# Routers of two sparse mixtures: gates on raw rows by tokens, mean and rstd applied to the logits, selection on logits, normalising on ScalarE

## The reference

```
# layer 1                                    # layer 3
logits = x @ gate_w + gate_b                 probs = softmax(x @ router_w.T)
vals, idx = top_k(logits, 2)                 gates, idx = top_k(probs, 2)
weights = softmax(vals)                      gates = gates / sum(gates)
h = relu(x @ w1[e] + b1[e])                  h = silu(x @ w1[e].T) * (x @ wgate[e].T)
out += weight * (h @ w2[e] + b2[e])          out += gate * (h @ w2[e].T)
```

## Time and profile before

| | us |
|---|---|
| median of three runs | 1674.88 |
| the profiled execution's own time | 1678.03 |
| span of its trace | 1676.3 |
| TensorE busy | 1599.8 (95%) |
| VectorE busy | 1241.1 (74%) |
| ScalarE busy | 932.0 (56%) |
| GpSimd busy | 290.5 (17%) |
| mean granted clock of TensorE | 0.984 |

### The profile page before, as it was taken

The page is one execution under the profiler, slowest core; times in us unless marked ns, Lnnn a source line. Parts: engine busy times, 40 slices in busy tenths (PEclk is TensorE's granted clock), DMA queues, the critical chain, the costliest instruction groups (busy, mean ns, idle before and its releaser), DMA issues.

```text
span 1676.3 us, 26239 instructions
## 1 busy us (share of the span) xinstructions
PE 1599.8 (95%) x8693; PEld 1247.8 (74%) x8693; DVE 1241.1 (74%) x2118; ACT 932.0 (56%) x1568; POOL 290.5 (17%) x270
## 2 busy tenths in 40 slices
PE   9998998999999998989999999999899999999998
PEld 8886766868866886468778765775588888888886
DVE  8827662464755474779999868552699999999997
ACT  1424473443624362139999744421387887887884
POOL 0014630010210021159100301000380000000003
PEclk9998997999999999989999999999999999999999
DMA  8010000022000002143853340005153528935003
GB/s 333 20 50 2 1 2 13 1 114 76 2 26 13 1 2 80 47 144 138 308 206 136 87 164 1 1 1 225 41 189 141 206 93 370 380 143 234 25 19 99
DMA packets 42240, 173.15 MB, mean 103 GB/s; under 512 B 10219, under 2 KB 10472, under 8 KB 26681
## 3 DMA queue, kind: packets, MB, share of 16 engines
q1 hardware_dynamic: 28742, 153.75, 23.9%
q0 software_dynamic: 8960, 10.29, 2.3%
q10 hardware_dynamic: 4464, 8.13, 1.3%
HBM read 275.54 MB, written 19.25 MB: 176 GB/s over the span
## 4 chain that ended last, share of the span: by engine, by line
PE 77%; DVE 13%; issue 3%; DMA 2%; ACT 2%; POOL 1%; SPq 0%; DVEq 0%; ACTq 0%; POOLq 0%
PE bank L1065 10%; PE bank L1069 10%; PE bank L1066 10%; PE bank L829 5%; PE bank L917 4%; PE bank L889 4%; PE bank L964 3%; PE bank L877 3%; PE bank L1013 3%; PE bank L1189 3%; PE bank L1297 3%; PE bank L848 2%; PE bank L1091 2%; PE bank L1271 2%; PE bank L840 2%
## 5 line engine op out<-in xcount | busy, mean ns | idle before, releaser
L710 POOL DMA_INDIRECT sb_W<-slots_out,sb_slus x20 | 29.9, 1494 | 541.7 <-DMA slots_out<-sb_rC 536.2
L785 PE MATMUL bank<-sb_ones 128*128 128x512 f32 x220 | 106.4, 634 | 8.8 <-DVE sb_rC L2584 6.3
L1505 ACT ACTIVATE sb_rF<-sb_rF,sb_nmx 125x625 f32<-125x625 f32 (+4 forms) x120 | 89.5, 746 | 45.1 <-DVE sb_nmx L2031 45.0
L652 POOL TENSOR_TENSOR sb_rstd<-sb_ve,sb_half 125x3 f32<-125x3 f32 (+3 forms) x23 | 22.9, 998 | 458.3 <-DVE sb_ve L1951 239.9
L384 DVE TENSOR_TENSOR sb_rA_r<-sb_W,sb_rA_r 128x1024 fp32r<-128x1024 f32 x68 | 83.5, 1227 | 12.2 <-ACT sb_rA_r L1602 12.0
L2031 DVE CUSTOM_DVE_ANT_0 sb_rF<-bank,sb_rG 125x625 f32<-125x625 f32 x80 | 61.5, 807 | 36.1 <-PE bank L877 35.2
L785 PEld LDWEIGHTS bank<-sb_ones 128*128 128x128 f32 x220 | 43.3, 203 | 59.9 <-issue 50.7
L384 DVE TENSOR_TENSOR sb_XT_r<-sb_W,sb_XT_r 128x1024 fp32r<-128x1024 f32 x68 | 83.4, 1226 | 0.0
L384 DVE TENSOR_TENSOR sb_rB_r<-sb_W,sb_rB_r 128x1024 fp32r<-128x1024 f32 x68 | 83.3, 1225 | 0.0
L1602 ACT ACTIVATE sb_rA_r<-sb_W 128x1024 fp32r<-128x1024 f32 x68 | 71.6, 1053 | 20.2 <-DMA sb_W<-in_w_m 17.5
L1637 ACT ACTIVATE sb_rG_r<-bank 128x512 fp32r<-128x512 f32 x51 | 30.6, 599 | 82.4 <-PE bank L1091 82.4
(11 more groups left out here) (534 smaller groups left out, 4780.1 us busy)
## 6 DMA issues: line engine op xcount, KB each, us to landing
sb_W<-in_w_m SPq DMA_DIRECT2D x204, 1024.0 KB
sb_rDE<-in_w_m SPq DMA_DIRECT2D x17, 1024.0 KB
sb_rC<-slots_in SPq DMA_DIRECT2D x33, 256.0 KB, 2.7
sb_W<-in_w_g SPq DMA_DIRECT2D x8, 1024.0 KB, 5.0
slots_out<-sb_rC ACTq DMA_DIRECT2D x31, 256.0 KB, 2.1
slots_in<-sb_rC SPq DMA_DIRECT2D x1, 4608.0 KB, 24.8
sb_W<-in_w_a SPq DMA_DIRECT2D x4, 1024.0 KB, 18.2
sb_W<-in_w_m SPq DMA_DIRECT2D x2, 2048.0 KB, 16.7
```

The costliest lines, as they stand in the source:

```text
L785: pe.matmul(bank[:, b, :], ones[:], ones[:, 0:1].broadcast_to([P, D]), start=True, stop=True)
L1505: act.activation(SM[:, s % 4, 0:kn], SM[:, s % 4, 0:kn], ACT.Exp, scale=-1.0, bias=nmx[:, s:s + 1], accum_out=dens[:, s:s + 1]).then_inc(S ...
```

## The change

For layers 1 and 3 alone:

- TensorE turns the raw rows `X` (`raw_gates`). Tile u's gates follow as soon as tile u is in `XT`, with tile u's 125 columns of `XT` standing still and the 8 columns of `gw` moving, so logits come out as rows. ScalarE copies all five tiles (`raw_tiles`).
- At router 0 TensorE multiplies ones by `gw` for the column sums, and VectorE keeps them in `gsum`.
- VectorE's `picks` takes out mean times `gsum`, multiplies by rstd, adds the bias (layer 1), and looks for the two best on the logits. The sums of `MK` wait for `MK` and no longer for `COMB`; exp takes LG minus the maximum, and `COMB` is made of exp and `MK`.
- ScalarE writes `XN` behind exp (`normal_rows`), and GpSimd's scatter waits for it.
- `chosen_nodes` goes tile by tile, each waiting for its tile of `SEL0`.
- VectorE's first low halves move behind `slots`; in stage 1 ScalarE's second high halves move ahead of `combT`.

```diff
+        gsum = sb("gsum", [R, 32])
...
-                pool.wait_ge(S("ln_vec"), LN[4 if r == 1 else 8] + STATS + T)
+                pool.wait_ge(S("x0"), ROWS_XN[r] + T)
...
+            def raw_gates(r, ready, base):
+
+                for t in range(T + 1):
+                    if t < T:
+                        pe.wait_ge(ready, base + t + 1)
+                        for c in range(C):
+                            mm = pe.transpose(bank[:, t, c * R:(c + 1) * R], X[:, t, c * P:(c + 1) * P], ident[0:R, 0:R])
+                        mm.then_inc(S("tr_full"), 1)
+                    if t >= 1:
+                        u = t - 1
+                        pe.wait_ge(S("x0"), ROWS_XT[r] + u + 1)
+                        for c in range(C):
+                            mm = pe.matmul(bank[0:R, 7, u * E:(u + 1) * E], XT[:, c, u * R:(u + 1) * R], gw[:, c, GW[r]:GW[r] + E],
+                                           start=(c == 0), stop=(c == C - 1))
+                mm.then_inc(S("rt_pe"), 1)
...
-                pe.wait_ge(S("rt_vec"), ROUTED[r] + ROUTER_OPS[r])
+                pe.wait_ge(S("rt_vec"), ROUTED[r] + PICKED[r])
...
-                def chosen_nodes(chosen):
-
-                    for k in range(C):
-                        for t in range(T):
+                def chosen_nodes(chosen, one_by_one=False):
+
+                    for t in range(T):
+                        if one_by_one:
+                            pe.wait_ge(S("sl_vec"), SLOT_OPS * (r // 2) + SELECTED - T + t + 1)
+                        for k in range(C):
                             mm = pe.matmul(bank[:, 6, k * P:(k + 1) * P], XN[:, t, k * P:(k + 1) * P], chosen(t),
-                                           start=(t == 0), stop=(t == T - 1))
+                                           start=(t == 0 and k == 0), stop=(t == T - 1), skip_group_check=True)
                     mm.then_inc(S("b_xt"), 1)
...
+                if c == 3:
+                    for k in range(C):
+                        pe.matmul(bank[0:R, 2, 0:32], ones[:, 0:R], gw[:, k, 0:32], start=(k == 0), stop=(k == C - 1))
...
-            routed_feats(4, 5, 1)
-            feats_ready(5)
+            raw_gates(1, S("lf_vec"), LF_OPS)
+            keep(5, 4)
...
+            def raw_tiles(r):
+
+                for t in range(T):
+                    act.wait_ge(S("tr_full"), T * (5 if r == 1 else 9) + t + 1)
+                    act.activation(XT[:, :, t * R:(t + 1) * R], bank[:, t, 0:C * R].rearrange("p (c n) -> p c n", c=C),
+                                   ACT.Copy).then_inc(S("x0"), 1)
+
+            def normal_rows(r):
+
+                act.wait_ge(S("ln_vec"), LN[4 if r == 1 else 8] + STATS + 1)
+                for t in range(T):
+                    act.activation(XN[:, t], X[:, t], ACT.Identity, scale=rstd[0:R, t:t + 1], bias=shift0[:, t:t + 1]).then_inc(S("x0"), 1)
...
-                act.wait_ge(S("rt_vec"), ROUTED[r] + (4 if r in (0, 2) else 3))
+                act.wait_ge(S("rt_vec"), ROUTED[r] + (5, PICKED[1] + 1, 4, PICKED[3] + 1)[r])
...
+                    normal_rows(3)
                     return
                 if r == 1:
-                    act.wait_ge(S("rt_pe"), 4 * r + 4)
+                    normal_rows(1)
+                    high_halves(1, ("a", 1), 0)
+                    act.wait_ge(S("rt_pe"), RT_PE[r] + 2)
...
-            feats(5, XT)
+            raw_tiles(1)
             high_halves(1, ("a", 0), 0)
-            logits(1)
             router(1)
-            high_halves(1, ("a", 1), 0)
...
+                if r == 0:
+                    c(dve.tensor_copy(gsum[:], bank[0:R, 2, 0:32]))
...
+            def picks(r):
+
+                k = 4 if r == 1 else 8
+                c = Chain(dve, S("rt_vec"), ROUTED[r])
+                means = bcast(mv[0:R, :, 0], E)
+                c(dve.tensor_tensor(EX[:], means, gsum[:, GW[r]:GW[r] + E].unsqueeze(1).broadcast_to([R, T, E]), ALU.mult))
+                c.sync()
+                dve.wait_ge(S("rt_pe"), RT_PE[r] + 1)
+                c(dve.tensor_tensor(LG[:], bank[0:R, 7, 0:T * E].rearrange("p (t e) -> p t e", t=T), EX[:], ALU.subtract))
+                c.sync()
+                dve.wait_ge(S("pow"), POW[f"ln{k}"])
+                c(dve.tensor_tensor(LG[:], LG[:], bcast(rstd[0:R, :], E), ALU.mult))
+                dve.scalar_tensor_tensor(out=shift0[:], in0=mv[0:R, :, 0], scalar=-1.0, in1=rstd[0:R, :], op0=ALU.mult,
+                                         op1=ALU.mult).then_inc(S("ln_vec"), 1)
+                c.sync()
+                if r == 1:
+                    c(dve.tensor_tensor(LG[:], LG[:], rbias[0:R, RB[r]:RB[r] + E].unsqueeze(1).broadcast_to([R, T, E]), ALU.add))
+                    c.sync()
+                for t in range(T):
+                    c(dve.max(m8[:, t], LG[:, t]))
+                c.sync()
+                for t in range(T):
+                    c(dve.max_index(i8[:, t], m8[:, t], LG[:, t]))
+                c.sync()
+                c(dve.tensor_copy(if8[:], i8[:]))
+                c.sync()
+                for k in range(2):
+                    c(dve.tensor_tensor(EQ[:, k], iota8[0:R].unsqueeze(1).broadcast_to([R, T, E]),
+                                        if8[:, :, k:k + 1].broadcast_to([R, T, E]), ALU.is_equal))
+                c.sync()
+                c(dve.tensor_tensor(MK[:], EQ[:, 0], EQ[:, 1], ALU.add))
+                assert c.n == ROUTED[r] + PICKED[r]
+                c(dve.tensor_tensor(LG[:], LG[:], m8[:, :, 0:1].broadcast_to([R, T, E]), ALU.subtract))
+                c.sync()
+                dve.wait_ge(S("rt_act"), RT_ACT[r] + 1)
+                c(dve.tensor_tensor(COMB[:], EX[:], MK[:], ALU.mult))
+                c.sync()
+                c(dve.tensor_reduce(red[:, 2], COMB[:], AX.X, ALU.add))
+                c.sync()
+                c(dve.reciprocal(red[:, 2], red[:, 2]))
+                c.sync()
+                c(dve.tensor_tensor(COMB[:], COMB[:], bcast(red[:, 2], E), ALU.mult))
+                assert c.n == ROUTED[r] + ROUTER_OPS[r]
...
-            normalise(n, 4, X)
-            feats(5, XT)
+            picks(1)
+            slots(1)
             low(dve, 1, ("a", 0), 0, part(PLACE[1]["a", 0]))
-            router(1)
-            slots(1)
```

78 lines of the change are left out of this document (33 added, 45 removed).

## The result

| | before | changed |
|---|---|---|
| median of the timed runs, us | 1676.45 (16 runs) | 1680.45 (16 runs) |
| lowest to highest, us | 1672.48 to 1680.73 | 1677.52 to 1684.10 |
| ratio, 95% interval | | 1.0026 (1.0017 to 1.0036) |
| span of the profiled execution, us | 1676.3 | 1678.2 |
| its own time, us | 1678.03 | 1679.93 |

By the ratio the changed kernel is slower by about 4.4 us (the medians differ by 4.0). The forecast was 1674.2, its range 1670.6 to 1678.2: outside, and of the wrong sign. A ratio of 0.001 is 1.7 us in all that follows.

What follows compares the result with a forecast made beforehand. TensorE, 77% of the chain, was taken as the bound, with savings only where it waits around the routers. +0.8 + 1.0 - 2.5 = -0.7 us, from a median of 1674.88, made 1674.2; range 1670.6 to 1678.2.

Steps and rivals of the forecast that it cites:

- Router 0, +0.8: Router 0: 8 added records and VectorE's copy lengthen the chain by 0.8 us, bounds +0.5 and +1.1.
- Stage 1, +1.0: Router 1: biases and chosen nodes start 1.3 us later behind ScalarE's queue; with the clock between -1.2 and +3.4, taken +1.0.
- Stage 3, -2.5: Router 3: chosen nodes start earlier, gain 5.2 us at full clock; a clock fall returns 2.2 to 5.0, taken -2.5.
- lead returned: Rival, chance 0.08: first blocks wait for weights or scattered nodes, stage 3 gives 0, sum +1.8, 1676.7 us.
- the scatter moves with the slots: Argument against the rival in which the first blocks wait for weights or scattered nodes and stage 3's lead is lost.
- A block loop whose length has changed: Sign named beforehand, in the block loops, that would show the prediction wrong; no size given.
- The two stages' falls: Stages 1 and 3: clock expected to fall within the raw gates, costing 2.1 us there and up to 2.9 in padding.
- the 0.80 for a padding record at the lower level: Price of a TensorE padding record at clock 0.50: 0.80 us (4.00 / 5), against 0.436 at full clock.
- upper edge of +2.5: Slow end of the forecast's own range for the whole kernel, -3.7 to +2.5 us.
- The slower rival: Rival, chance 0.13: ScalarE's queue ahead of combT with the lower clock decides, +4.3 us, 1679.2.
- the gates can start only when the padding of 17 is over: Stage 1: raw gates start at 701.8 us, though X is ready tile by tile before.

Runs made afterwards that it cites:

- after_last_between: The changed kernel with tile gsum allocated behind all others and VectorE's two low halves between selection and slots, in both stages; ratio to before 1.0006.
- gsum_alone: The kernel before with only the sums of the gates added at router 0, tile gsum at the changed kernel's place; ratio 1.0047, run once more 1.0033.
- tile_only: The kernel before with the tile gsum (128 bytes a partition) allocated at the changed kernel's place and never used, no instruction added; ratio 1.0008.
- gsum_last: The kernel before with the sums of the gates (products and copy) added and tile gsum allocated behind all others; ratio 1.0008.
- padding_between: after_last_between with the four padding products behind the raw gates moved to between their tiles, in both stages; ratio to before 1.0032.
- early_gates: after_last_between with gsum's products moved into stage 1's padding, and padding ahead of raw gates cut: 8 products instead of 16, none instead of 6; ratio to before 0.9913.

## Why the prediction was wrong

- **Router 0, +0.8.** From the first gate to VectorE's sum with the bias it is 6.88 us instead of 5.65, +1.2 at full clock, a little above the upper bound of 1.1. The whole stretch took +0.22 in the profiled pair, whose stretches at the lower level lie otherwise (before 283.2 to 290.0, changed 284.3 to 287.7 and 294.6 to 298.0). Taking the sums away again was worth 0.0010, which is within the intervals. The term was near, and no run sizes it better.
- **Stage 1, +1.0.** +0.50 in the trace. The queue on ScalarE was as described, but each link was a little faster: logits 7.2 us behind the first transposes, not 7.6, selection 2.75, not 3.0. So combT was ready at 717.17, and the biases started, with the shift of the whole trace (0.83) taken out, when they had before, not 1.3 us later. The lead of 1.06 at step 0 came from the clock: biases and chosen nodes took 9.9 us instead of 10.9, since less of them lay at the lower level. It went again in the low stretch of steps 0 and 1, which kernels without raw gates have too.
- **Stage 3, -2.5.** To step 0 it was -2.48. Step 1 gave 1.85 back. This is the step that failed first: "the low halves moved behind the slots on VectorE (two of about 1.2) lie in the wait for chosen nodes". They did, for TensorE; GpSimd's scatter was beside them. The rival "lead returned" (chance 0.08) named this end, and I argued against it with "the scatter moves with the slots". The rows had VectorE's queue, but no row of GpSimd's issues stood beside it.
- **No term at all for the tile.** I priced instructions and waits, and the diff's first line, a tile allocated ahead of others, at nothing without saying so. It moved every later tile by 128 bytes, which cost 0.97 and 0.27 us in the loops of the traces and, in seven of eight, 1.4 to 2.1 more at the gathers. The tile ahead together with the sums at router 0, which had a term, made ratios of 1.0047 and 1.0033 with none of the new routers. The tile's place and that of the low halves are all that sets the changed kernel (1.0026) apart from after_last_between (1.0006). "A block loop whose length has changed" stood among the things that would prove me wrong, and it had.
- **The clock, sized from single falls.** The two stages' falls were foreseen (it came within the gates in stage 3, just behind them in stage 1), and priced by the records that they lengthen. The loss is broader: the mean clock of the timed runs is 0.981 to 0.982 in all seven kernels with a raw router and the late gates, 0.983 to 0.985 in the five with several runs that have none. 0.003 is up to 5 us. Of this the two traces show little (0.984 and 0.982), for the profiled execution of before was itself 1.6 us above the median of 16 runs (1678.03 and 1676.45). Its clock was read as the typical one. Two numbers of the prediction are weaker than they look: the 0.80 for a padding record at the lower level is a mean over five of which the first began at full clock (the next four start 0.85 apart), and the forecast's own upper edge of +2.5 stands there without a sum. That the clock is lower with raw gates is shown; why it is also lower in gsum_alone (0.9835 and 0.9827) than in tile_only and gsum_last (0.9848 and 0.9841) is not.
- **The slower rival** (0.13, 1679.2) had nearly the right time and the wrong mechanism: ScalarE's queue decided nothing.
- Not settled: in which stretches the lower clock falls in the runs without a trace. In stage 3 the low time is 6.8 to 13.7 us in the six traces with its raw gates late, and 3.4 to 6.8 without; stage 1 varies more between traces of like kernels (10.2 to 17.1, and 20.5 in padding_between) than between kinds.

The padding that the change left in place hid its use. Raw gates need only X, tile by tile, while the padding ahead of them was sized for XN, after all moments. The prediction noted this ("the gates can start only when the padding of 17 is over") and took it as fixed; the 14.5 us of early_gates lie there, 13.1 of them in the two stretches from the turning of the rows to step 0.
